# Second expert product: the tile of the middle layer outermost, both row halves inside, and the split middle rows awaited pair by pair

## The reference, cut to what matters

```python
h = gelu(x @ w1[e] + b1[e])      # 256 -> 1024
y = h @ w2[e] + b2[e]            # 1024 -> 256
```

## Time and profile before

| | us |
|---|---|
| median of 3 runs | 3193.83 |
| profiled execution | 3193.49 |
| its span | 3191.9 |
| first mixture's expert loop | 548 to 1010 |
| second mixture's expert loop | 2865 to 3145 |
| TensorE busy with matmuls | 2464.4 |
| VectorE busy | 2027.2 |
| ScalarE busy | 1513.9 |

### The profile page before, as it was taken

How to read it: one execution, slowest core, us unless ns; L and a number is a source line. 1 busy time by engine, 2 the same in 40 slices (tenths; PEclk the granted TensorE clock), 3 DMA queues, 4 the chain that set the end, 5 groups by cost and what they waited for, 6 DMA issues and landing times. The chain is left out here.

```text
span 3191.9 us, 54522 instructions
## 1 busy us (share of the span) xinstructions
PE 2464.4 (77%) x20856; PEld 1905.0 (60%) x20856; DVE 2027.2 (64%) x2826; ACT 1513.9 (47%) x2617; POOL 1195.8 (37%) x674
## 2 busy tenths in 40 slices
PE   0399940888885199946699999999999998308883
PEld 0288830888885188846366666666666664308882
DVE  7954440777775554463677777777777772327773
ACT  0233320666663143334166666666666665206661
POOL 0100005000002500011188888888888887230003
PEclk9999955999998599978599999999999999559996
DMA  9865303555553465426200000030000000125552
GB/s 408 355 238 174 110 6 134 206 213 208 207 207 105 137 245 174 129 87 195 68 14 15 12 13 15 13 79 15 15 10 15 13 13 1 43 106 203 207 207 98
DMA packets 140109, 375.94 MB, mean 118 GB/s; under 512 B 22032, under 2 KB 82704, under 8 KB 121872
## 3 DMA queue, kind: packets, MB, share of 16 engines
q1 hardware_dynamic: 122928, 319.82, 28.4%
q0 software_dynamic: 15696, 48.77, 4.2%
q10 hardware_dynamic: 1296, 4.75, 0.4%
HBM read 314.30 MB, written 58.98 MB: 117 GB/s over the span
## 5 line engine op out<-in xcount | busy, mean ns | idle before, releaser
L1255 DVE TENSOR_REDUCE at_part_max<-ps_x 128x2 f32<-128x1024 f32 x624 | 734.2, 1221 | 265.1 <-PE ps_x L1158 265.1
L1105 POOL TENSOR_TENSOR at_pool_sum<-at_pool_sum,at_probs 128x1024 f32<-128x1024 f32 x364 | 866.1, 2380 | 95.8 <-ACT at_probs L1226 54.7
L1226 ACT ACTIVATE at_probs<-ps_s 128x512 f32<-128x512 f32 x1352 | 698.4, 603 | 340.9 <-PE ps_s L1120 307.2
L1120 PE MATMUL ps_s<-at_qst,at_kst 97*128 97x256 f32 x2704 | 518.7, 312 | 5.2 <-ACT at_probs L1226 4.6
L1120 PEld LDWEIGHTS ps_s<-at_qst,at_kst 97*128 97x128 f32 x2704 | 369.8, 190 | 218.5 <-ACT at_probs L1226 115.7
L461 PE MATMUL ps_acc<-adj_hi,y_hi 128*128 128x512 f32 (+1 forms) x728 | 280.0, 385 | 230.8 <-DVE adj_lo L508 230.8
L1137 PE MATMUL ps_oz<-at_probs,k_xhat 128*32 128x256 f32 (+1 forms) x5408 | 392.1, 386 | 0.0
L508 DVE TENSOR_TENSOR adj_lo<-adj_raw,adj_hi 128x1024 fp32r<-128x1024 f32 (+1 forms) x182 | 207.6, 1148 | 239.5 <-ACT adj_hi L430 239.5
L430 ACT ACTIVATE adj_hi<-adj_raw 128x1024 fp32r<-128x1024 f32 (+1 forms) x182 | 181.9, 1000 | 305.7 <-PE ps_acc L463 278.9
L830 POOL DMA_DIRECT2D results<-ex_res x54 | 38.8, 719 | 723.4 <-DVE ex_res L817 723.4
L732 PE MATMUL ps_ex_o<-ex_w_hi,ex_hid_hi 128*128 128x256 f32 x864 | 244.9, 283 | 76.0 <-DVE ex_hid_lo L811 69.7
(11 more groups left out here) (181 smaller groups left out, 4048.3 us busy)
## 6 DMA issues: line engine op xcount, KB each, us to landing
ex_w<-w SPq DMA_DIRECT2D x108, 1024.0 KB, 6.7
adj_raw<-adjT SPq DMA_DIRECT2D x156, 512.0 KB, 4.2
adj_rows<-adj SPq DMA_DIRECT2D x26, 1664.0 KB, 11.0
slots<-zeros POOLq DMA_DIRECT2D x27, 512.0 KB, 21.5
ex_rows<-slots SPq DMA_DIRECT2D x54, 256.0 KB, 2.9
results<-ex_res POOLq DMA_DIRECT2D x54, 256.0 KB, 2.8
at_qst<-qk_parts SPq DMA_DIRECT2D x78, 128.0 KB, 2.5
ex_b<-b SPq DMA_DIRECT2D x54, 128.0 KB, 2.1
```

Of the source, the lines that this page charges most:

```text
L1105: pool.tensor_tensor(pool_sum[:, g % 2], pool_sum[:, g % 2], probs[:, tile % RING], ALU.add).then_inc(pool_added, 1)
L1120: last = pe.matmul(ps_s[:, unit % S_BANKS, hh, :], kst[:, 2 * j + hh, k * P:(k + 1) * P], qst[:, g % 2, 2 * j + hh, :], start=True, stop=True)
L1226: act.activation(probs[:, tile % RING, 2 * j:2 * j + 2], ps_s[:, unit % S_BANKS], ACT.Exp, scale=scale).then_inc(taken, 1)
L1255: dve.tensor_reduce(part_max[:, g % 2, heads, qt, kc], ps_x[:, pair, :], AX.X, ALU.max).then_inc(x_free, 1)
```

## The change

In the second product the loop over the tiles `h` of the middle layer becomes the outer one and the loop over the row halves `a` the inner one. The one wait for all four pairs is replaced by a wait for pair `h // 2` ahead of each even `h`. The matmuls themselves, their operands, the start and stop flags of the two sums and all other engines' code are the same.

```diff
                 pe.wait_ge(out_made, n + 2)
-                pe.wait_ge(hidden_lo, n * PAIRS + 2 * PAIRS)
                 pe.wait_ge(weights_lo, n * 2 + 6)
-                for a in range(TT):
-                    for h in range(HT):
+                for h in range(HT):
+                    if h % 2 == 0:
+                        pe.wait_ge(hidden_lo, n * PAIRS + (PAIRS + h // 2 + 1))
+                    for a in range(TT):
                         at, rows_at = slice(h * D, (h + 1) * D), slice(a * P, (a + 1) * P)
                         last = three(ps_o[:, a, 0:D], hid_hi[:, h, rows_at], hid_lo[:, h, rows_at],
                                      w_hi[:, k, 1, at], w_lo[:, k, 1, at], h == 0, h == HT - 1)
```

## The result

The changed kernel takes 3113.82 us (median of 4 runs, 3113.19 to 3114.82) against 3193.62 us before: ratio 0.9752, 95% interval 0.9736 to 0.9769, 79.8 us less. The forecast was 3105 us with a range of 3096 to 3124. The time fell as forecast and lies in the range, 9 us above the point.

The account below looks back on a forecast made before the run. TensorE, with one hole per chunk, was taken to bound the expert loop. Saving 1.64 us in each of 54 chunks gives 88.6 us off 3193.49, so 3105 us was predicted, with a range of 3096 to 3124.

Parts of the forecast that it names:

- The stall: Ahead of the second product: TensorE waits for the last pair though pair 0 is ready; starting earlier saves 1.54 us per chunk.
- What is late next: At the next chunk's start: `w_lo` is ready 0.6 us before TensorE needs it, the thinnest margin, so nothing becomes late.
- Rival (b): At the chunk boundary: TensorE stops for `w_lo`, losing 0.3 us per chunk, 16 us in all: 3121 us; chance 0.08.
- The added waits: Second product, four waits for pairs: all met before TensorE arrives, taken as nothing, bounded by 0.4 us per chunk, 22 us.
- the loop order: Second product: output bank changes after every 3 matmuls, not 24; taken as nothing, with at most 18 us gained.
- Rival (c): Second product: changing the output bank after every 3 matmuls stalls TensorE; at 0.15 us each 25 us slower, 3218; chance 0.03.
- Rival (d): Expert loop: the clock falls to its lower level for 48 matmuls per chunk, 171 us more, 3364 us; chance 0.01.
- The restart: Second product's first matmul: the longer gap after it, 0.21 us where 0.11 is usual, goes with the stall, saving 0.10 us per chunk.
- The pace: Both products: matmuls keep following each other every 0.1134 to 0.1138 us, within a new chunk period of 11.36 us.
- rival (a): Expert loop: the filled hole brings the slower 0.1176 us matmul pace to 42 more chunks, costing 17 us: 3122; chance 0.10.

## Why the prediction was right, and where it was off

**The stall.** Right, and all of it. The 76.0 us went to 0.0, and the two kernels that take the change apart show that the waits pair by pair are the whole cause (3113.52 with the old order, 3192.22 with the new order and one wait).

**What is late next.** Right: nothing. `ex_w_lo` holds TensorE for the same 9.8 us as before at the two stage starts, VectorE catches up within the chunk, the weights land in time. Rival (b) did not happen.

**The added waits and the loop order.** Right at nothing. Rival (c), the bank, did not happen: the order alone left the time where it was (ratio 0.9992), and with the old order the pace is the slow one all the same. Rival (d), the lower clock, did not happen: the granted clock stays at 1.00 in the window above, the upper level. What the Trainium skill, "TensorE: Matmul & The Clock Gate", section "A second HAM failure mode: psum-queue depth-cycling", tells of another kernel, a clock that swings because the engine is idle between groups while it cycles through PSUM banks, does not happen in this loop: TensorE is busy for 23.50 of 23.50 us there.

**The restart.** I let 0.10 us per chunk go with the stall. It did not: behind the transposes the first matmul is followed by a gap of 0.20 us even without a wait. But the product starts 0.35 us after the first transpose, not 0.46. The two errors cancel (0.55 against 0.57 us). From the first transpose to the second matmul of the product it was 610.50-608.29 = 2.21 us and is 0.55: 1.66 us closed per chunk, 1.64 forecast.

**The pace.** This is the term that was off: "The new period is 5.44+0.46+5.46" takes the matmuls at 0.1134 to 0.1138 us, and they came at 0.1177 to 0.1179. It is what rival (a) described, with a chance of 0.10. Against that rival the prediction held that 33 chunks of the first stage run without the slow pace; that is true of their second products alone. In every second chunk the 24 matmuls behind the table load's gap were slow before the change too, and of the 0.25 us by which those chunks were longer only 0.16 was the gap; 0.10 was this pace. Over two chunks 192-24 = 168 matmuls slowed: 168 x 0.0043 = 0.72 us more. The gap shrank from 0.16 to 0.07 us, since a slower TensorE needs its fifth tile later: 0.09 less. The spot behind the transposes is 0.04 less. That is 22.97+0.59 = 23.56, as measured. Rival (a)'s price of 17 us for 42 chunks left this out; with 20 chunks at 0.10+0.09 less it is 13.

**The sum by stage.** From the first hidden matmul to the last `ex_res` the first stage went from 448.9 to 402.5 us, 46.4 less, where 34 x 1.64 = 55.8 was forecast. The second went from 268.2 to 238.1, 30.1 less, where 32.8 was forecast; its second products were already slow in 9 of 19 chunks (the prediction had read about 11 of 20), so there the new pace costs less. The two make 76.5, 12.1 less than the 88.6 forecast; the spans differ by 79.4. The 2.9 us outside the loops have no edit behind them and lie within the spread of the runs of before (3189 to 3195). It is luck that they bring the total to within 9 us of the point.

**What stays open.** What decides between the two paces. It is not the output bank, zeros in one operand, or the fullness of the stream. What the traces show is where it changes. Behind a short pause with no transposes ahead of it the fast pace turned slow: 58 of 58 times at the fifth hidden tile, and 40 of 45 times at the start of the first product in the kernel without transposes. Where the second product follows the first with no transposes between them, the pace mostly flips: in 51 of 54 chunks of that kernel, and in 22 of the 24 last chunks of a stage in the other twelve kernels with the transposes in their old place, whether the hole there is 2.1 us or none. Behind the transposes without a hole it is nearly always slow. There a pause makes the fast pace likely and does not force it: in the second stage of the kernel before it is slow behind the same hole of 1.99 us in 9 chunks of 19. I have no mechanism for it, and no kernel here holds the fast pace for free.

## What to carry to other kernels

Where an engine waits for the last of several pieces, compare the time at which each piece is ready with the time at which it is needed in the consumer's own pace; here the waits alone, without any reordering, gave 2.5%. Measure the hole from start to start of the instructions around it, not by the wait view: that showed 1.39 us of 1.66. And when a hole in a pipelined engine is closed, do not carry over the pace measured next to the hole: look in the trace for stretches of the same instructions at another pace (here 3.8% slower, in 9 of 19 chunks of the second stage and behind the table load's gap in every second chunk of the first), and price the forecast for both.

## What the runs showed of the hardware that I had not expected

- The same 128x256 matmuls follow each other every 0.1134 or every 0.1177 us at the same granted clock of 1.00, mostly for a whole product at a time. Zero weights, and with them zero sums, run no faster than real ones (slow in 51 of 52 chunks).
- A gap of 0.16 us inside a fast first product left the rest of it slow, 58 of 58 times.
- From the first of four transposes of 128x128 to the second product it is 0.35 us, and the product's second matmul comes 0.20 us later, not 0.12.
- A wait of TensorE for the end of its own transposes makes that mostly 0.93 to 1.02 us, three times the 0.35 without it.
- The table load of 1.28 us can be moved into ScalarE's idle time by a one-element activation of 0.20 us, and it was worth nothing that the ratios show here (0.9743 against 0.9752).
